# A third slot for w2, squares in quarters, and two feed-forward blocks moved ahead of the statistics

## What is computed

```python
x_flat = layernorm(x).reshape(-1, 1024)
gates = top2_softmax(x_flat @ router_w)            # zero but for two experts
h   = gelu(einsum('nd,edf->enf', x_flat, w1) + b1)   # D 1024 -> FF 4096
out = einsum('enf,efd->end', h, w2) + b2             # FF -> D
res = x_flat + out
mu, var = mean(res), mean((res - mu)**2)             # over D, per expert
expert_out = (res - mu) * rsqrt(var + 1e-6) * gamma + beta
y = einsum('end,ne->nd', expert_out, gates)
```

## Time and profile before

| | |
|---|---|
| median of the 2 runs shown | 6440.97 us (6246.29 and 6635.64) |
| profiled execution | 6232.85 us |
| its span, slowest core | 6231.1 us (fastest core 6176.6) |
| granted PE clock, mean of the cores | 0.863 to 0.868 of full speed |
| PE busy | 4464.8 us (72%) |
| DVE busy | 1801.7 us (29%) |
| ACT busy | 1058.1 us (17%) |
| POOL busy | 120.8 us (2%) |
| chain that ended last | PE 61%, DVE 16%, DMA 14%, issue 3%, ACT 3% |
| matmuls of phase B (L818) | 1946.8 us busy, 389.6 us idle before them |
| matmuls of phase A (L769) | 1814.8 us busy, 257.1 us idle before them |

### The profile page before, as it was taken

One profiled execution on the slowest core, in us unless ns is written; L12 is line 12 of the kernel. 1 busy time (PEld: TensorE's weight loads), 2 busy tenths in 40 slices (PEclk: granted clock), 3 DMA queues, 4 the chain that ended last, 5 costly groups with the idle time before them and its releaser, 6 DMA issues.

```text
span 6231.1 us, 49901 instructions; the slowest of 8 cores (6176.6 to 6231.1 us)
## 1 busy us (share of the span) xinstructions
PE 4464.8 (72%) x18680; PEld 1892.0 (30%) x19040; DVE 1801.7 (29%) x2381; ACT 1058.1 (17%) x1297; POOL 120.8 (2%) x167
## 2 busy tenths in 40 slices
PE   1663332488887787878787852879798988979893
PEld 0221111233333333333333321334343433434341
DVE  1445553303131212222222235012224041313225
ACT  0221111212121111111121200212112030312110
POOL 0000000000000000000000000000000000000000
PEclk9776666789898898989898975989899999989896
DMA  5000004174737463647373621122222313122221
GB/s 69 27 27 27 14 14 81 43 167 109 161 108 159 110 155 103 157 107 160 104 163 107 149 78 68 65 98 92 84 102 75 118 61 118 69 94 98 78 98 48
DMA packets 229019, 586.59 MB, mean 94 GB/s; under 512 B 75056, under 2 KB 75184, under 8 KB 220592
## 3 DMA queue, kind: packets, MB, share of 16 engines
q1 hardware_dynamic: 157568, 444.95, 20.6%
q0 software_dynamic: 71216, 138.44, 14.2%
HBM read 570.77 MB, written 150.99 MB: 116 GB/s over the span
## 4 chain that ended last, share of the span: by engine, by line
PE 61%; DVE 16%; DMA 14%; issue 3%; ACT 3%; SPq 1%; DVEq 0%; ACTq 0%; POOLq 0%
PE pall L769 28%; PE pall L818 23%; DMA w2buf<-w2s_scr 6%; DMA w2buf<-w 6%; PE pall L399 4%; DVE res_b L827 3%; DVE rs_r L225 3%; PE pall L872 1%; PE pall L857 1%; PE pall L326 1%; DMA yacc<-xmid_scr 1%; ACT sq_b L863 1%; SPq L191 1%; PE pall L462 1%; DMA xmid_scr<-x_f 1%
## 5 line engine op out<-in xcount | busy, mean ns | idle before, releaser
L818 PE MATMUL pall<-h_b,w2buf 128*128 128x512 bf16 x8032 | 1946.8, 397 | 389.6 <-DMA w2buf<-w 218.1
L769 PE MATMUL pall<-xn_b,w1buf 128*128 128x512 bf16 x8016 | 1814.6, 387 | 257.1 <-ACT h_b L775 241.6
L818 PEld LDWEIGHTS pall<-h_b,w2buf 128*128 128x128 bf16 x8192 | 805.3, 101 | 1531.2 <-issue 731.5
L769 PEld LDWEIGHTS pall<-xn_b,w1buf 128*128 128x128 bf16 x8192 | 810.8, 99 | 1264.7 <-issue 339.9
L827 DVE SCALAR_TENSOR_TENSOR res_b<-pall,b_c,xn_b 128x512 bf16<-128x512 f32 x256 | 192.2, 751 | 2896.9 <-PE pall L818 2872.4
L775 ACT ACTIVATE h_b<-pall,b_c 128x512 bf16<-128x512 f32 x1024 | 701.8, 687 | 1097.7 <-PE pall L769 1097.5
L863 ACT ACTIVATE sq_b<-res_b 128x4096 bf16<-128x4096 bf16 x32 | 115.7, 3616 | 2513.8 <-DVE res_b L827 2436.0
L399 PE MATMUL pall<-xn_b,WdWi_b 128*128 128x512 bf16 x1000 | 234.7, 397 | 150.5 <-DVE x_f L373 72.4
L914 DVE TENSOR_TENSOR sq_b<-res_b,pall 128x512 f32<-128x512 bf16 x256 | 176.1, 688 | 378.9 <-PE pall L903 353.2
L299 PE MATMUL pall<-ident,xt 128*128 128x128 f32 x256 | 52.7, 363 | 217.8 <-DMA xt<-ssm_x 110.8
L919 DVE SCALAR_TENSOR_TENSOR yacc<-sq_b,fgam_c,yacc 128x512 f32<-128x512 f32 x256 | 192.2, 751 | 27.4 <-DVE sq_b L916 0.9
(11 more groups left out here) (103 smaller groups left out, 1299.5 us busy)
## 6 DMA issues: line engine op xcount, KB each, us to landing
w2buf<-w2s_scr SPq DMA_DIRECT2D x384, 512.0 KB, 3.3
w1buf<-w POOLq DMA_DIRECT2D x32, 2048.0 KB, 16.6
w1s_scr<-w1buf SPq DMA_DIRECT2D x32, 2048.0 KB, 6.7
w2buf<-w POOLq DMA_DIRECT2D x128, 512.0 KB, 6.4
w2s_scr<-w2buf SPq DMA_DIRECT2D x128, 512.0 KB, 4.2
w1buf<-w1s_scr SPq DMA_DIRECT2D x32, 2048.0 KB, 8.1
xt<-ssm_x SPq DMA_DIRECT2D x8, 2048.0 KB, 8.8
xmid_scr<-x_f SPq DMA_DIRECT2D x4, 2048.0 KB, 7.4
```

The lines of the kernel that those rows point to most:

```text
L769: e.matmul(bank(b_), l, rr, start=(kk == 0), stop=(kk == FC - 1)))
L818: e.matmul(bank(m2), l, rr, start=(kk2 == 0), stop=(kk2 == 31)))
```

## The change

1. `w2buf` gets three slots of 2048 columns in place of two; slot, release and store tokens go by the round modulo 3. The prefetch distance in the program stays one step.
2. `sq_b` has half its former size. The squares are formed in four operations of 2048 columns in place of two of 4096, each after the sum matmuls of the one before; this holds for every expert and for the norm at each group's start. `tscr` moves to the start of `sq_b`.
3. Block 0 of the next expert is emitted right behind the residual eviction, ahead of the gate transposes and the statistics matmuls; before, it stood behind the rows.
4. Block 1 of the next expert is emitted behind the last square matmuls and ahead of `rows_combine`; before, it stood behind the apply. Blocks 2 and 3 stay behind the apply. The last expert of a group has no next one and keeps its order.

```diff
--- before.py
+++ after.py
@@ -526,11 +526,11 @@
     xn2_b = ef(nc.sbuf_tensor("xn2_b", [128, FC * GT], BF16))
     yacc = ef(nc.sbuf_tensor("yacc", [128, FC * GT], F32))
     res_b = ef(nc.sbuf_tensor("res_b", [128, FC * GT], BF16))
-    sq_b = ef(nc.sbuf_tensor("sq_b", [128, FC * GT // 2], BF16))
+    sq_b = ef(nc.sbuf_tensor("sq_b", [128, FC * GT // 4], BF16))
     w1buf0 = ef(nc.sbuf_tensor("w1buf0", [128, FC * 1024], BF16))
     w1buf1 = ef(nc.sbuf_tensor("w1buf1", [128, FC * 1024], BF16))
-    w2buf = ef(nc.sbuf_tensor("w2buf", [128, 2 * 2048], BF16))
-    tscr = sq_b[:].bitcast(F32)[:, GT:2 * GT]
+    w2buf = ef(nc.sbuf_tensor("w2buf", [128, 3 * 2048], BF16))
+    tscr = sq_b[:].bitcast(F32)[:, 0:GT]
     out_tok = [h_b[:].bitcast(F32)[:, i * D:(i + 1) * D] for i in range(2)]
     w1bufs = (w1buf0, w1buf1)
 
@@ -542,7 +542,7 @@
     w1_round = [0]
     w1_free = [None, None]
     w1_slot_store = [None, None]
-    w2_slot_store = [None, None]
+    w2_slot_store = [None, None, None]
     w1s_tok = {}
     w2s_tok = {}
 
@@ -570,10 +570,10 @@
         return tok, par
 
     w2_round = [0]
-    w2_free = [None, None]
+    w2_free = [None, None, None]
 
     def prefetch_w2(ee, kb, g, th):
-        par = w2_round[0] % 2
+        par = w2_round[0] % 3
         r.wait("q", w2_free[par])
         r.wait("y", w2_free[par])
         r.wait("q", w2_slot_store[par])
@@ -631,22 +631,22 @@
                 r.emit("t", lambda e, rr=rhs, fc=fc, nt=nt: e.matmul(
                     pall[0:1, nt * 512: nt * 512 + 512],
                     ones_col_b[:], rr, start=(fc == 0), stop=(fc == FC - 1)))
-        for half in range(2):
+        for half in range(4):
             r.wait("s", xmb_v)
+            if half > 0:
+                r.wait("s", r.token("t"))
             r.emit("s", lambda e, half=half: e.activation(
-                sq_b[:], res_b[:, half * 4 * GT:(half + 1) * 4 * GT], AF.Square))
+                sq_b[:], res_b[:, half * 2 * GT:(half + 1) * 2 * GT], AF.Square))
             sqh_s = r.token("s")
             r.wait("t", sqh_s)
             for nt in range(2):
-                for fc in range(4):
+                for fc in range(2):
                     rhs = sq_b[:, fc * GT + nt * 512: fc * GT + nt * 512 + 512]
-                    fcg = half * 4 + fc
+                    fcg = half * 2 + fc
                     r.emit("t", lambda e, rr=rhs, fcg=fcg, nt=nt: e.matmul(
                         pall[0:1, 1024 + nt * 512: 1024 + nt * 512 + 512],
                         ones_col_b[:], rr,
                         start=(fcg == 0), stop=(fcg == FC - 1)))
-            if half == 0:
-                r.wait("s", r.token("t"))
         ln2_mm_t = r.token("t")
         r.wait("v", ln2_mm_t)
         ps_sum_row = pall[0:1, 0:1024]
@@ -831,6 +831,10 @@
                     bank_free[m2] = r.token("v")
             res_v = r.token("v")
 
+            last_in_group = ee == n_experts - 1
+            if not last_in_group:
+                emit_A_ms(ee + 1, 0)
+
             r.wait("t", gates_v)
             r.wait("t", bank_free[6])
             r.wait("t", bank_free[7])
@@ -857,26 +861,29 @@
                     r.emit("t", lambda e, rr=rhs, fc=fc, nt=nt: e.matmul(
                         pall[0:1, nt * 512: nt * 512 + 512],
                         ones_col_b[:], rr, start=(fc == 0), stop=(fc == FC - 1)))
-            for half in range(2):
+            for half in range(4):
                 r.wait("s", res_v)
                 r.wait("s", prev_est_t)
+                if half > 0:
+                    r.wait("s", r.token("t"))
                 r.emit("s", lambda e, half=half: e.activation(
-                    sq_b[:], res_b[:, half * 4 * GT:(half + 1) * 4 * GT],
+                    sq_b[:], res_b[:, half * 2 * GT:(half + 1) * 2 * GT],
                     AF.Square))
                 sqh_s = r.token("s")
                 r.wait("t", sqh_s)
                 for nt in range(2):
-                    for fc in range(4):
+                    for fc in range(2):
                         rhs = sq_b[:, fc * GT + nt * 512: fc * GT + nt * 512 + 512]
-                        fcg = half * 4 + fc
+                        fcg = half * 2 + fc
                         r.emit("t", lambda e, rr=rhs, fcg=fcg, nt=nt: e.matmul(
                             pall[0:1, 1024 + nt * 512: 1024 + nt * 512 + 512],
                             ones_col_b[:], rr,
                             start=(fcg == 0), stop=(fcg == FC - 1)))
-                if half == 0:
-                    r.wait("s", r.token("t"))
             est_t = r.token("t")
             prev_est_t = est_t
+
+            if not last_in_group:
+                emit_A_ms(ee + 1, 1)
 
             r.wait("v", est_t)
             r.wait("v", prev_ebc_t)
@@ -891,10 +898,6 @@
                 u2_rb[0:1, :], nm_r[0:1, :], g_r[0:1, :], ALU.mult))
             r.emit("v", lambda e: e.tensor_copy(g_rb[0:1, :], g_r[0:1, :]))
             urows_v = r.token("v")
-
-            last_in_group = ee == n_experts - 1
-            if not last_in_group:
-                emit_A_ms(ee + 1, 0)
 
             r.wait("t", urows_v)
             for nt in range(2):
@@ -932,7 +935,7 @@
                 bank_free[b_] = y_v
 
             if not last_in_group:
-                for ms in range(1, 4):
+                for ms in range(2, 4):
                     emit_A_ms(ee + 1, ms)
                 h_done_s = r.token("s")
                 a_mm_tok = r.token("t")
```

## The result

The changed kernel is faster: the ratio of its time to that of before is 0.962, with a 95% interval of 0.959 to 0.965, some 236 us less. Its profiled execution's span is 6021.6 us against 6231.1. (The plain medians, 6428.01 and 6247.55 us, also hold runs in which a whole die ran at a lower clock, with either kernel; the ratio leaves them out.)

What follows compares the result with a forecast made beforehand. TensorE was taken to bound the kernel, losing time by standing, restarting at the lower clock and waiting for weights in group 0. Terms of -232 - 85 - 12 + 6 = -323 against 6232.85 gave 5910 us, range 5800 to 6060.

Steps and rivals of the forecast that it cites:

- Term 1: Third w2 slot in group 0's eight th = 0 phase B passes: 99 us shortens to 70, gain 232 us.
- rival 4: Third w2 slot does nothing because a queue's order holds the load anyway: 6227 us, chance 0.03.
- The formula: Group 0, th = 0 pass: 13 steps of 4.5 us plus start, issue, landing and last matmuls, 68.5 us, taken as 70.
- rival 2: Transfers in group 0's th = 0 passes limit sooner, share 0.9: gain 96 instead of 232, 6046 us, chance 0.12.
- the forecast case: Whole kernel's time lands between 5850 and 5975 us, around the forecast of 5910; chance 0.62.
- Term 2: Third slot in the 24 phase B passes from the bf16 copy: waits go, gain 85 us, bounds 60 and 88.
- Term 3: Reordered seam between experts, 14 times: the stop moves from block 0 to the broadcast, net gain 12 us.
- The rule on micro-idles: Statistics stretch: frequent micro-idles between matmul groups make the clock fall; some 5 us more per seam, seam sum +58.
- Term 4: Norm at each group's start: the same quartered squares with nothing beside them, a cost of 6 us.
- The apply's cover: Before phase B: blocks 2 and 3 alone must cover the 52.9 us apply, with a margin of 5 us.
- the wait for the float32 w2: Sign in phase B: TensorE's wait for this load falls from 218 us to under 70.
- The DMA share of about 0.95: Sign in group 0's th = 0 passes: the DMA share rises to about 0.95 and they last about 70 us.

Runs made afterwards that it cites:

- the halves kernel: Squares in two halves again, g_rb sharing the bytes of mu_r, against the changed kernel; ratio to before 0.9546, 47 us below the changed kernel.
- store_none: Every w2 store of group 0 left out, against the changed kernel; group 0's th = 0 passes took 57.6 us.
- mid_block: rows_combine and the three rows emitted in the middle of block 1, against the changed kernel; ratio 0.939, 146 us below the changed kernel.

## Why the prediction was right, and the term that was off

The direction, the size within the range and the order of the terms were right: 5910 us was forecast, a gain of 323 us, and the gain is about 236.

- **Term 1, forecast 232 us, measured 8 x 15.4 = 123.** The mechanism was right and the size was off, in the baseline and in the new pass.
  - The baseline was one long pass: the 99 us between the earlier trace rows and the end was expert 2's, while the mean over passes and cores is 92.9. That is 6.1 x 8 = 49 us.
  - The new pass was forecast at 70 us and took 77.4, 59 us in all. Of these 7.4 us, 77.4 - 73.0 = 4.4 are the hold: a slot stays bound until its store has landed, 6.7 us. The prediction looked at this only as rival 4 (the third slot does nothing) and dismissed it whole.
  - The other 3 us are the step. The prediction took 4.9 us of engine time and divided it by the share of 1.09 of a load alone, 4.5 us. Loads and stores mixed reach 1.03 to 1.04 and take 5.2 us of engine time, 5.0 us per step.
  - The formula is 2 us too long and otherwise holds: 13 steps of 5.0 us and 10 us around them make 75, and 73.0 was measured without the hold; 12 steps make 70, and 67.9 was measured with four slots.
  - The case that came true lies between the forecast and rival 2. The step of rival 2, 4.9 / 0.9 = 5.4 us, is the mean of the changed kernel, and its pass of 87 us was too long because it had 16 such steps in it, although three kb lie in SBUF at the start. The term was 109 us too large. That puts the result (6023 us profiled, 5997 by the ratio) above the 5850 to 5975 of the forecast case; it lies in the stated range because this reached over the term's bounds, which is as much caution as understanding.
- **Term 2, forecast 85, measured 37 + 29 + 29 = 95.** The mechanism was right: the 7 us of cover swallow the landing, and the wait falls from 88.0 to 6.7 us. The gain is 14 us more than the wait, and over the upper bound of 88, which counted nothing but the wait. No run shows where the rest comes from.
- **Term 3, forecast -12, measured -18**, and by its parts: the stop of 12.9 us is gone; block 0 waits 4.49 (forecast 4.5); the squares' waits come to 103.2 us (forecast 105); the new wait is 8.9 us (forecast 9.0). Block 0 takes 29.8 us and blocks 1 and 2 28.6 and 29.4 against a full pace of 27.4, so the clock costs 2.4, 1.2 and 2.0 (forecast 2, 1.9 and 2.5). With the quarters in it the reordered seam nearly cancels itself, as forecast; alone, the moves gave 1%.
- **The rule on micro-idles** in the Trainium skill ("TensorE: Matmul & The Clock Gate", A second HAM failure mode: psum-queue depth-cycling). The rows of the seam after agree with it in direction: of the four square groups the first two take 1.03 and 1.02 us, the last two 1.86 each, so the second of the 2.15 us gaps did cost the higher clock. The 5 us per seam that the prediction put beside the rule were its own estimate, and far too high: the halves kernel has one gap in place of three, and of its 3.3 us per seam 0.7 is the clock.
- **Term 4, forecast 6.** With the quarters in the two last seams (5 us of the 44) the forecast for the groups' ends was 11 us; measured 7 + 3 + about 3 at the first norm, 13.
- **The apply's cover** held: phase B has no wait on L927, with blocks 2 and 3 as its only cover. The margin is 5.5 us, where 5 was forecast:

```profile
5496.95 0.75 DVE L927 SCALAR_TENSOR_TENSOR yacc<-pall,fbet_c,yacc 128x512 f32<-128x512 f32 x1 [0.46 <-DVE yacc L922]
...
5503.17 17.00 PE L818 MATMUL pall<-h_b,w2buf 128*128 128x512 bf16 x78 [1.03 <-ACT h_b L775]
```

Of the signs that the prediction named, one failed: the wait for the float32 w2 fell to 138 us and not to under 70. The DMA share of about 0.95 came true as a mean, but it went with passes of 77 us and not 70.

## What to carry to other kernels

One more buffer removes a wait only down to the next limit. Work out both limits that a third slot meets, the slot's whole round (load, use and everything else that holds the slot, here a store) and the traffic, and take the traffic's pace from a stretch in which the same mixture of transfers is already dense, not from a transfer alone. A baseline should be a mean over all passes, not the one that the timeline showed first.

When a block of work is moved to hide a stop, look at what the in-order engine beside it must now do first: here the square root came to stand behind 16 gelus, and putting it between the eighth and the ninth gave 146 us, more than the moves alone had given (a ratio of 0.990).

## What the runs showed of the hardware

- A float32 load that converts to bf16 wrote 186 GB/s in one burst of 2 MB, but in a stream of 512 KB loads with nothing beside it the 16 engines were at a share of 0.95 for 146 GB/s (store_none), at a pace that TensorE set. Mixed with as many bytes of stores the sum is 209 to 218 GB/s, not the 253 that the two rates alone would give.
- A table load on ScalarE between two functions took 1.28 us, and the next operation began 0.02 us after it: switching to the square root and back cost ScalarE 3.6 us with the square root in it (mid_block).
- Three gaps of 2.15 us with about 1 us of matmuls between them brought the clock down at the third group of four matmuls; a single gap of 2.06 us in a dense stream had not the earlier trace rows.
